# A state-space layer, gated linear attention and routed experts on one core: decay masks spread by DMA and finished on ScalarE, in place of masks summed on TensorE

## The reference

```
x  : [16, 512, 128]
x  = norm(x + state_space(x));  x = norm(x + x @ sign(W).T)
q, k, v = x @ Wq.T, x @ Wk.T, x @ Wv.T            # 16 heads of 64
g  = -softplus(x @ Wd.T + bd)                     # log decay, one number per token and head
k  = k * sigmoid(x @ Wg.T)
s_t = exp(g_t) * s_{t-1} + k_t^T v_t ;  o_t = q_t s_t         # per head, over the 512 tokens
out = rms_norm(o) * norm_w * sigmoid(x @ Wog.T);  x = norm(x + out @ Wo.T)
x  = norm(x + top-2-of-8 experts(x))
```

## Time and profile before

| | before |
|---|---|
| median of 3 runs | 2624.32 us (2620.51 to 2631.4) |
| the profiled execution, its own time | 2623.08 us |
| its span, first to last instruction | 2621.2 us |
| mean granted clock of TensorE | 0.936 of full |
| PE busy, share of the span | 2279.5 us, 87% |
| DVE busy | 1866.8 us, 71% |
| ACT busy | 1354.7 us, 52% |
| POOL busy | 818.0 us, 31% |
| DMA moved | 189.63 MB |

### The profile page before, as it was taken

One profiled execution on the slowest core, in us unless ns is written; L12 is line 12 of the kernel. 1 busy time (PEld: TensorE's weight loads), 2 busy tenths in 40 slices (PEclk: granted clock), 3 DMA queues, 4 the chain that ended last, 5 costly groups with the idle time before them and its releaser, 6 DMA issues. The chain is left out here.

```text
span 2621.2 us, 53454 instructions
## 1 busy us (share of the span) xinstructions
PE 2279.5 (87%) x17080; PEld 1685.0 (64%) x17081; DVE 1866.8 (71%) x3521; ACT 1354.7 (52%) x2568; POOL 818.0 (31%) x1092
## 2 busy tenths in 40 slices
PE   3499999999989898989898989898989939999990
PEld 1257565666667575757575757575757739999990
DVE  2795868686868677777777686858694437777777
ACT  2265656555655555565656555646564513333334
POOL 0111414141414141414232323322332333333336
PEclk9598999999999999999999989989999969999995
DMA  4431414141323232322222232313140022122216
GB/s 125 118 89 38 105 38 97 38 98 45 91 57 80 69 82 55 86 60 76 65 70 69 66 76 59 88 47 85 46 99 11 14 97 87 54 57 59 60 46 192
DMA packets 144249, 189.63 MB, mean 72 GB/s; under 512 B 17001, under 2 KB 92785, under 8 KB 143681
## 3 DMA queue, kind: packets, MB, share of 16 engines
q1 hardware_dynamic: 121808, 119.18, 15.5%
q0 software_dynamic: 22272, 67.92, 12.2%
HBM read 110.23 MB, written 27.56 MB: 53 GB/s over the span
## 5 line engine op out<-in xcount | busy, mean ns | idle before, releaser
L1405 DVE TENSOR_TENSOR_SCAN hs<-decay,push 128x512 f32<-128x512 f32 x256 | 354.4, 1406 | 23.8 <-ACT decay L1075 18.2
L984 PE MATMUL banks<-rowsT,w_here 128*128 128x128 f32 x2176 | 269.9, 278 | 5.9 <-DVE w_here L1729 5.8
L1503 DVE TENSOR_TENSOR S<-banks,S 128x512 f32<-128x512 f32 x256 | 164.2, 683 | 148.1 <-PE banks L804 143.5
L984 PEld LDWEIGHTS banks<-rowsT,w_here 128*128 128x128 f32 x2176 | 256.4, 194 | 9.3 <-issue 9.0
L1510 DVE SCALAR_TENSOR_TENSOR oT<-tog,banks 128x512 f32<-128x512 f32 x128 | 87.5, 684 | 238.2 <-ACT sq L1128 237.8
L1808 POOL DMA_DIRECT2D y<-ch x96 | 88.6, 923 | 512.0 <-DVE ch L1413 403.7
L1906 POOL TENSOR_TENSOR qd<-q,qd 128x512 f32<-128x512 f32 x96 | 134.5, 1401 | 302.5 <-ACT qd L1146 302.5
L1949 POOL DMA_INDIRECT results_scratch<-rows_out,result_to x136 | 131.9, 970 | 240.3 <-ACT rows_out L1283 233.3
L1108 ACT ACTIVATE S<-banks 128x512 f32<-128x512 f32 x272 | 162.4, 597 | 74.3 <-PE banks L792 48.0
L1272 ACT ACTIVATE tanh_h<-banks 128x512 f32<-128x512 f32 x136 | 81.3, 598 | 202.9 <-PE banks L984 168.9
L772 PE MATMUL banks<-x2T,w_k 128*128 128x512 f32 x256 | 138.1, 621 | 49.2 <-DVE k L1496 49.2
(11 more groups left out here) (222 smaller groups left out, 5540.5 us busy)
## 6 DMA issues: line engine op xcount, KB each, us to landing
y<-ch POOLq DMA_DIRECT2D x96, 512.0 KB
b_all<-bc_scratch SPq DMA_DIRECT2D x128, 256.0 KB, 5.3
c_all<-bc_scratch SPq DMA_DIRECT2D x128, 256.0 KB
rows_in<-rows_scratch SPq DMA_DIRECT2D x136, 66.0 KB
both<-results_scratch SPq DMA_DIRECT2D x32, 256.0 KB, 3.4
w<-w_dram SPq DMA_DIRECT2D x3, 2048.0 KB, 8.0
x_tok<-x_dram SPq DMA_DIRECT2D x16, 256.0 KB, 4.0
x_again<-x_dram SPq DMA_DIRECT2D x16, 256.0 KB, 3.0
```

The source lines that it names most:

```text
L984: mm = pe.matmul(bank_h[:, u % 2, n, here], w_here[:, u % 2, n, here], x, start=True, stop=True)
L1405: nc.vector.tensor_tensor_scan(hs[:, h, :], decay[:, n % 2, h, :], push[:, h, :], 0.0, ALU.mult, ALU.add).then_inc(s_scan, 1)
L1503: nc.vector.tensor_tensor(S[:, g, :], full(ring, f"S{g}_{c}", j), S[:, g, :], ALU.mult).then_inc(ring.free_sem(f"S{g}_{c}"), 1)
```

## The change

PE no longer makes masks. `fall` has 16 rows (heads in the order half, odd, pair), the three bf16 parts, the matrices of ones and PE's products of them are gone. Instead:

- SP stores `fall` and exp(-`fall`) of the whole sequence to DRAM (`store_falls`), then spreads for each stage 8 rows of 128 numbers over the 128 partitions, straight into one of the four slots of `S` (512 KB a stage, `spread_falls`), and, for chunks 1 to 3, exp(-F) over the partitions of `q_fall` (two DMAs of 128 KB a stage).
- POOL adds `hide` (1e30 in the future, 512 KB) into the slot with an accumulating DMA (`hide_future`). The first four are issued in units 4 and 5, the others three stages ahead.
- ACT takes exp(-x + F_j) of the slot, the F_j as a bias for each partition, one instruction a head: eight of 128x128 a stage, in place. `fall_tok` has the bias, turned by PE as before.
- POOL multiplies q by `q_fall` into `qd`; the exp of it on ACT is one instruction for the whole sequence (`exp_falls`, unit 3).

Beside this the second load of x goes into `x1` itself and waits for the end of the sign layer; `take` copies into a buffer of its own (`x2_kept`), so that the wait for the scattered rows moves from ACT to DVE's `residual(0)`; `x3T` lies in `kd`; POOL's `sum_state` of a stage comes after the queries, the mask and the scatters; `store_x3` comes one state later on SP.

```diff
@@ tables
-FALL_PARTS = (3, 4, 5)
+FALL_EXP = 3
+MASK_SLOTS = 4
+MASK_AHEAD = 3
+MASKS_IN_UNIT = {4: (0, 1), 5: (2, 3)}
-SIZES_STAGE, BC_STAGE, TAKE_STAGE, X3_AFTER = 7, 3, 2, 3
+SIZES_STAGE, BC_STAGE, TAKE_STAGE, X3_AFTER = 7, 3, 2, 4
+FALLS_AFTER = 3
+SPREAD_AFTER = {3: (0, 1, 2, 3), 6: (4,), 7: (5, 6, 7)}
@@ SP body
-                        drained(sp, ring, i - 1, "mix")
-                    sp.dma_start(x_again[:], x_dram[bass.ds(i, 1)].rearrange("b p c d -> (b p) c d")
+                        drained(sp, ring, i - 1, "ffn")
+                    sp.dma_start(x1[:], x_dram[bass.ds(i, 1)].rearrange("b p c d -> (b p) c d")
...
+                for m in range(STATES):
+                    if i is not None:
+                        spread_bc(m, i)
+                    if j is not None:
+                        if m == FALLS_AFTER:
+                            store_falls(j)
+                        if m == X3_AFTER and not first(j):
+                            store_x3(j - 1)
+                        for h in SPREAD_AFTER.get(m, ()):
+                            spread_falls(h, j)
...
+            def store_falls(j):
+
+                sp.wait_ge(s_fall, at(j, TILES, TILES))
+                sp.dma_start(fall_dram[bass.ds(j, 1)].rearrange("b c h n -> (b h) c n"),
+                             fall[:].rearrange("h (c n) -> h c n", n=P)).then_inc(s_fall_stored, 16)
+                sp.wait_ge(s_fall_exp, at(j, 1, 1))
...
+            def spread_falls(h, j):
+
+                c, f = divmod(h, 2)
+                heads = slice(8 * f, 8 * f + 8)
+                slot = h % MASK_SLOTS
+                if h == 0:
+                    sp.wait_ge(s_fall_stored, at(j, 16, 16))
+                if h >= MASK_SLOTS:
+                    sp.wait_ge(s_O, at(j, STAGES, h - MASK_SLOTS + 1))
+                sp.dma_start(S[:, slot].rearrange("p o n -> p (o n)"),
+                             fall_dram[bass.ds(j, 1), c, heads, :].rearrange("b h n -> b (h n)").broadcast_to([P, 8 * P])
+                             ).then_inc(s_fall_spread[slot], 16)
+                if c == 0:
+                    return
+                if h == 2:
+                    sp.wait_ge(s_fall_exp_stored, at(j, 16, 16))
+                if h >= 4:
+                    sp.wait_ge(s_qd, at(j, STAGES - 2, h - 3))
...
@@ PE front
-                if c:
-                    bank, full = fill(ring, f"e{f}_{c}", j)
-                    for t in range(4):
-                        mm = pe.matmul(bank[:, t * P:(t + 1) * P], nselpair[:, 4 * f + t, :],
-                                       fall_parts[:, here], start=True, stop=True)
-                    mm.then_inc(full, 1)
...
-                if h == 0:
-                    pe.wait_ge(s_fsplit, at(j, 5, 5))
-                mask(2 * f, c, j)
-                mask(2 * f + 1, c, j)
                 scores(f, c, j)
@@ ACT front
-                    nc.scalar.activation(chunk_fall[:, pairs], falls[:, :, P - 1], ACT.Exp).then_inc(s_kept, 1)
-                    nc.scalar.activation(qd[:, pairs, :], falls, ACT.Exp).then_inc(ring.free_sem(f"e{f}_{c}"), 1)
+                    nc.scalar.copy(chunk_fall[:, pairs], q_fall[:, f, P - 1::P]).then_inc(s_kept, 1)
...
-                for g in (2 * f, 2 * f + 1):
-                    drain(S[:, g, :], f"D{g}_{c}", j, ACT.Exp)
+                slot = h % MASK_SLOTS
+                act.wait_ge(s_hidden[slot], at(j, 16 * STAGES // MASK_SLOTS, 16 * (h // MASK_SLOTS + 1)))
...
+                for odd in range(2):
+                    for t in range(4):
+                        here = S[:, slot, odd, t * P:(t + 1) * P]
+                        row = c * HEADS + 8 * f + 4 * odd + t
+                        ins = nc.scalar.activation(here, here, ACT.Exp, scale=-1.0, bias=fall_tok[:, row:row + 1])
+                    ins.then_inc(s_mask, 1)
@@ POOL
+            def hide_future(h, j):
+
+                slot = h % MASK_SLOTS
+                pool.wait_ge(s_fall_spread[slot], at(j, 16 * STAGES // MASK_SLOTS, 16 * (h // MASK_SLOTS + 1)))
+                pool.sem_inc(s_hide_begun, 1)
+                nc.gpsimd.dma_start(S[:, slot].rearrange("p o n -> p (o n)"), hide[:], accum_op=ALU.add
+                                    ).then_inc(s_hidden[slot], 16)
...
-                if m is not None and m <= SUMS:
-                    sum_state(m, i)
                 if j is not None:
                     if 2 <= h + 1 < STAGES:
                         decay_queries(h + 1, j)
+                    if MASK_SLOTS <= h + MASK_AHEAD < STAGES:
+                        hide_future(h + MASK_AHEAD, j)
                     if h % 2 and h > 1:
                         rms_of((h - 3) // 2, j, j)
                     if not first(j) and h in SCATTERS:
                         send_rows(j - 1, h)
                 if i is not None:
+                    if m is not None and m <= SUMS:
+                        sum_state(m, i)
```

More of the change, by code:

```diff
@@ L20 @@
 FCHUNKS = FF // P
-PART2, PART3, DT_ROW, ROWS = 64, 96, 32, 112
+DT_ROW = 32
 X_ROWS = DT_ROW + STATES
@@ L762, in log_decay @@
                 bank, full = fill(ring, "wd", j, "x2T")
-                pe.matmul(bank[0:ROWS, :], w_d[:], x2T[:], start=True, stop=True).then_inc(full, 1)
+                pe.matmul(bank[0:HEADS, :], w_d[:], x2T[:], start=True, stop=True).then_inc(full, 1)
             def project(u, j):
@@ L1084, in log_decay @@
             def log_decay(j):
-                nc.scalar.activation(sp_in[:], full(ring, "wd", j)[0:ROWS, :], ACT.Identity, bias=b_d[:]
+                nc.scalar.activation(sp_in[:], full(ring, "wd", j)[0:HEADS, :], ACT.Identity, bias=b_d[:]
                                      ).then_inc(ring.free_sem("wd"), 1)
                 drained(act, ring, j, "wd")
+                after(act, s_fall_exp_stored, at(j, 16, 0))
                 nc.scalar.activation(sp_ln[:], sp_in[:], ACT.Abs).then_inc(s_dsp, 1)
@@ L1095, in logs, with exp_falls @@
                 nc.scalar.activation(sp_ln[:], sp_ln[:], ACT.Ln, bias=1.0).then_inc(s_dsp, 1)
[L1097 to L1105 removed]
+            def exp_falls(j):
+                act.wait_ge(s_fall, at(j, TILES, TILES))
+                nc.scalar.activation(fall_exp[:], fall[:], ACT.Exp, scale=-1.0).then_inc(s_fall_exp, 1)
             def drain(dst, use, j, func=ACT.Copy, scale=1.0):
@@ L1172, in take @@
                 act.wait_ge(s_x2, at(j, TILES, TILES))
[L1173 to L1177 removed]
+                after(act, s_residual, at(j, TILES, 0))
+                nc.scalar.copy(x2_kept[:], x2_new[:]).then_inc(s_x2_taken, 1)
             def stage(h, i, j, n):
```

180 lines of the change are left out of this document (75 added, 105 removed).

## The result

| | before | after |
|---|---|---|
| median, beside each other on one chip (4 runs each) | 2622.64 us | 2741.22 us (2729.99 to 2773.64) |
| span of the profiled execution | 2621.2 us | 2728.1 us |

What follows compares the result with a forecast made beforehand. PE was taken to bound stages 3 to 7, DVE's order to end the first part. Gains of 2.0 + 5.0 = 7 us in 15 rounds (105), plus 12 and 3, took 120 us off 2623.08: forecast 2504 us, range 2420 to 2610.

Steps and rivals of the forecast that it cites:

- What PE loses: Mask and query products off PE in the stages: 12.8 us a round, 205 us in 16 rounds if all counted.
- 7 with half of the burst hidden and 10.9 with all of it: Gain a round by how much DMA time is hidden: forecast 2504 us, chance 0.50; rival 2446 us, chance 0.22.
- ACT: Masks on ACT: eight exps 2.5 us a stage, +10 us a round, -5 for exps and casts gone; off the path.
- DVE and POOL in the first part: Without POOL's `fall_rest`, scan pairs give DVE 2.7 us; push 4 alone would come at about 1046.3, not 1049.05.
- What the DMAs cost: First part: 3.6 MB at 218 GB/s bring `b_all` at 1051, stalling push 4 by 4.7 us; first part +0.6 us.
- slower rival: First part: DMAs delay push 4, or ACT at mask 0, until PE's gain is lost; 2668 us, chance 0.12.
- Mask 0 "hardly adds": First part: mask 0, 1 MB at half of 218 GB/s, lands near 1050 and adds hardly anything.
- Stages 0 to 2 keep 2.0, stages 3 to 7 keep 5.0: The us a round still gained in those stages from PE's relief, after the losses counted against it.
- PE's cold restart: After the first part: PE waits about 4 us for kd 0 and comes back slow, costing 1.2 us.
- PE's clock: Whole round: PE idles more, clock 0.90 in place of 0.97 stretches work 8 us; about 2620 us, chance 0.10.
- the clock of the stages under 0.95: Sign listed as showing the forecast wrong: PE's granted clock in the stages below this level.
- The last attention keeps 12, the start 3: Outside the 15 rounds: 12 us saved with no `b_all` to wait for, 3 us from loading 0.8 MB less.

Runs made afterwards that it cites:

- e1: Against after: SP asks for state 4's `b_all` right behind the stores of the falls, ahead of the mask spreads and `q_fall`; 2679.94 us.
- e2: Against after: the accumulating DMAs of `hide` left out, ACT waits for the spread alone, mask values not the reference's; 2608.12 us.
- e3: Against after: no spreads and no `hide` DMAs, ACT makes the exps from a constant tile, masks lack the decay values; 2480.20 us.
- e10: Against after: only POOL's stage order put back (sum, queries, rms, scatters, `hide` last), SP unchanged; 2665.81 us.
- e5: Against e1: POOL's stage order put back (sum, queries, rms, scatters, `hide` last); 2589.51 us.
- e12: Against e3: POOL's stage order as in e5, still without mask DMAs or decay values in the masks; 2487.01 us.
- e9: Against e6: SP's order at the stages mended, `hide` and `q_fall` of a stage together, state 7's `b_all` ahead of stage 4's `q_fall`; 2548.05 us.
- e8: With POOL's order of e5: masks 0 and 1 made on PE in f32, spreads of masks 2 and 3 behind states 4 and 5; 2622.58 us.
- e6: Against e5: SP lays `hide` first, POOL adds the spread, masks 0 and 1 ahead of the state's sum in unit 4; 2581.47 us.

## Why the prediction was wrong

**What PE loses: right in size, not in place.** The masks are gone, and without the DMAs in their place a round is 126.7 - 117.4 = 9.3 us shorter. The prediction had 7 with half of the burst hidden and 10.9 with all of it. But 5.0 of the 9.3 lie in the first part, where it had 3.9 at most, and 4.3 behind it, where it had 7 or more. That the two misses nearly cancel is luck.

**ACT: right.** Eight exps took 2.44 us, predicted 2.5.

**DVE and POOL in the first part: right.** Scans take 2.34 us in place of 3.70, and DVE was ready for push 4 at 1090.9 - 1055.5 = 35.4 us behind the copy; 1046.3 had been predicted in a round that began near 1010.

**What the DMAs cost: the step that failed first,** "Counting 0.7 MB of POOL's in that time". The rate was no worse than I took: 253 GB/s from 1079.8 to 1101.5, with the engines 1.04 busy, against 218. What was off is how much was moved before `b_all` was there: 5.48 MB in 21.7 us, where the sum had 3.6 MB in 16.5. The queues of that stretch:

```profile
DMA packets 1860, 5.48 MB, mean 253 GB/s; under 512 B 237, under 2 KB 285, under 8 KB 1860
q0 software_dynamic: 647, 2.36, 54.8%
q1 hardware_dynamic: 1213, 3.12, 49.5%
```

POOL's queue (q0) moved 2.36 MB where I had counted 0.7, and took half of the engine time. POOL's issues came when predicted (the sum 27.5 us and `hide` 0 29.8 us behind the copy, 0.4 us behind `b_all`); only their share was too small. So DVE waited 9.7 us a round, not 4.7. That is the slower rival's mechanism, but `b_all` was there 1101.5 - 1055.5 = 46 us behind the copy, short of the 48 (1058) from which that rival was to decide by itself. The first part is 4.3 us longer than in before, where 0.6 was predicted: 3.7 us of the miss. The kernel is slower than the rival's upper price (2668) because a second step failed, and by more. e1 and e2 each show one half of it: the queue ahead (SP), and the load beside (POOL). The Trainium skill, DMA: Bandwidth & Descriptors, section Issuing engines are not separate DMA queues, says that SP's and POOL's transfers share the engines; the trace agrees, 49.5 and 54.8% of them in one stretch, and I had named the rule without giving POOL its half in the sum.

**Mask 0 "hardly adds": right only while push 4 is later.** It was predicted to land 40 us behind the copy and landed at 41.3. Behind it come ACT's 2.44 us, and e1, where push 4 is in time, has the first product at 42.2 and not at 38.2. Repairing the queue alone could not have saved the forecast.

**Stages 0 to 2 keep 2.0, stages 3 to 7 keep 5.0: the second step that failed.** Behind the first product a round takes 86.5 us in after, 83.5 in before, where I had 7.6 less: 10.6 us of the miss. The prediction saw that POOL's order was changed and priced the wrong victim: it put 1.1 us on y's sum. What POOL's wait for a spread held up were the rms, for which DVE's residual waits (2.5 us a round). The changed order also put POOL's product of the queries beside DVE's `push`, 6.7 us a round in the stages in place of 3.7, but that stretch is there without the wait too (e2, e3). Putting POOL's order back gives about 5 us in after's stages (e10) and in e1's (e5), and little or nothing where there is no spread to wait for (e12). Another 2.7 us are the clock's (below). The 7.6 were too much even without the mask DMAs: in e3 what lies behind the first product gains only 4.3 us. Where a mask has some 25 us of room, it was right that the mask itself isn't late; the instructions behind the wait had no such room.

**PE's cold restart: right in kind.** Behind the 10.96 us of idle time two products for v took 2.08 us (1105.18), where two took 1.08.

**PE's clock: a rival whose condition came true.** It asked for 0.90 in place of 0.97 over a round, and after has 0.90 over the twelve rounds, where before has 0.96. The sign "the clock of the stages under 0.95" came true as well: 0.94 and 0.88 in the round shown. Its cause was wrong, since e3, in which PE has as little work and no mask DMA to wait for, is at 0.96: the clock fell with the waits that the DMAs brought (in stages 0 to 4 PE waits 16.4 us a round in after, 10.0 of them for `kd`, and 3.6 in e3). But it has a price of its own. In the rest of a round the other engines do the same at 24.1 us and 0.93 as at 30.0 and 0.72, and the mean there is 26.8, so 2.7 us a round, some 40 in all. In e9, where the waits are mended, the rest is at 0.79 and 28.6 us still. What PE did before the clock fell doesn't tell the two rounds apart: in both it waited 1.88 us for `x1T`. Why it falls in one and not in the other isn't shown.

**The last attention keeps 12, the start 3: wrong.** From the last x2T copy to the end there are 2728.1 - 2119.9 = 608.2 us, in before 2621.2 - 2017.7 = 603.5. No `b_all` is late there. Of DVE's waits behind POOL's rms, 3.8, 6.6 and 5.1 us, only the 6.6 is new (before has 3.6 and 5.1), and it is gone with POOL's order mended: e5 takes 598.7, e10 596.4. But e8, with the same order, takes 608.0 and e3 601.3, so the rest of it is open. The first copy comes 1.2 us later, not 3 earlier; over all the runs it comes between 129.2 and 133.0.

**What makes up the loss.** From e3 to after a round gets 16.6 us longer. The runs give 5.3 to `b_all` behind the burst (e1), 3.6 to the way of mask 0 (e5 to e6), about 5 to POOL's order (e5, e10); they are read from different stretches and needn't add up. Between e9, where these three are mended, and e3 lie 68 us still, 4.8 a round in the table: 0.1 in the first part, 2.2 in stages 0 to 4, where DVE waits 2.3 for `b_all`, and 2.5 in the rest. The last are mostly the clock's: the rest is below 0.83 in eight of e9's twelve rounds and in four of e3's, and takes 24.1 us in both kernels where the clock is 0.93. How much the DMAs' load as such costs wasn't separated.

## What to carry to other kernels

Work moved from a busy engine to DMAs is paid at the queue, not at the mean load: before such a move, list for each transfer on the path what is sent in front of it on its own queue and what the other queues send at the same moment, and give each of them its full share. Where one result takes two transfers in a row, do first the one that doesn't hang on the data (here the constant), so that only one is left behind the data (e6 did this together with two other changes, so its 3.6 us are not the order's alone). A wait put into an in-order engine is priced by the least patient instruction behind it, wherever its own result has room; and when a transfer is moved later, every wait for it has to move as well. Before a stretch of one kernel is compared with the same stretch of another, look at the granted clock of both: here it made 24 or 30 us of one and the same work.
